# A three-layer CIN recommender on one core: layer 0 run three chunks further ahead of layer 1, its h in a ring of four, five of its chunks in the opening, TensorE's loop written out four times

## The reference

```
h = inputs                                   # [1024, 39, 16]
for i in 0, 1, 2:
    x = einsum('bhd,bmd->bhmd', h, inputs)   # outer product over fields
    x = einsum('bcd,oc->bod', x, W_i) + b_i  # 200 outputs
    x = relu(x)
    h, direct = x[:, :100], x[:, 100:]       # layer 2: direct = x
score = (sum over 16 of the directs, dense layers) @ fc_W + fc_b + biases
```

## Time and profile before

| what | us |
|---|---|
| median of three runs | 2750.92 |
| lowest, highest of them | 2747.41, 2753.69 |
| the profiled execution, its own time | 2752.34 |
| its span in the trace | 2750.5 |
| PE busy in that span | 2649.5 (96%) |
| granted TensorE clock, mean | 0.992 of full |

### The profile page before, as it was taken

The page is one execution under the profiler, slowest core; times in us unless marked ns, Lnnn a source line. Parts: engine busy times, 40 slices in busy tenths (PEclk is TensorE's granted clock), DMA queues, the critical chain, the costliest instruction groups (busy, mean ns, idle before and its releaser), DMA issues.

```text
span 2750.5 us, 66670 instructions
## 1 busy us (share of the span) xinstructions
PE 2649.5 (96%) x17928; PEld 2640.2 (96%) x17928; DVE 2285.0 (83%) x4584; ACT 1834.6 (67%) x4776; POOL 2249.6 (82%) x1912
## 2 busy tenths in 40 slices
PE   0699999999999999999999999999999999999999
PEld 0599999999999999999999999999999999999998
DVE  2788888888888888888888888888888888888884
ACT  0576776766767667676777767677677766766663
POOL 6788888888888888888888888888888888877763
PEclk9799999999999999999999999999999999999999
DMA  8844545445444454544545455454554545545441
GB/s 149 199 124 123 133 126 130 124 118 144 116 133 125 118 149 112 136 121 122 146 111 138 120 131 137 114 136 118 138 131 118 133 117 140 129 117 136 111 115 51
DMA packets 199914, 349.82 MB, mean 127 GB/s; under 512 B 66632, under 2 KB 118697, under 8 KB 199615
## 3 DMA queue, kind: packets, MB, share of 16 engines
q1 hardware_dynamic: 185782, 342.81, 45.6%
q0 software_dynamic: 10496, 2.88, 3.1%
q10 hardware_dynamic: 3464, 2.68, 0.3%
HBM read 344.29 MB, written 14.17 MB: 130 GB/s over the span
## 4 chain that ended last, share of the span: by engine, by line
PE 94%; POOL 2%; SPq 2%; DVE 1%; issue 1%; DMA 1%; ACT 0%; POOLq 0%; ACTq 0%; DVEq 0%
PE acc L642 61%; PE acc L643 28%; PE acc L667 2%; POOL raw L498 1%; PE hrep L678 1%; DVE W L1061 0%; SPq L319 0%; DMA odd<-lin 0%; PE acc L742 0%; PE acc L743 0%; PE acc L744 0%; SPq L309 0%; DMA raw<-table,idx 0%; PE hrep L764 0%; PE hrep L766 0%
## 5 line engine op out<-in xcount | busy, mean ns | idle before, releaser
L642 PE MATMUL acc<-W,xhi_d 128*128 128x400 f32 x5632 | 1732.4, 367 | 17.2 <-DVE xlo_d L1087 10.6
L643 PE MATMUL acc<-W,xlo_d 128*128 128x200 f32 x5632 | 1434.9, 255 | 0.0
L1087 DVE TENSOR_TENSOR xlo_d<-prod_d,xhi_d 128x512 fp32r<-128x512 f32 (+1 forms) x1536 | 983.9, 641 | 205.1 <-ACT xhi_d L819 147.2
L1079 DVE TENSOR_TENSOR prod_d<-hrep,xrep 128x512 f32<-128x512 f32 (+1 forms) x1536 | 1039.0, 677 | 105.8 <-issue 27.7
L548 POOL TENSOR_TENSOR xlo_p<-prod_p,xhi_p 128x512 fp32r<-128x512 f32 (+1 forms) x768 | 953.8, 1242 | 181.3 <-ACT xhi_p L813 135.6
L642 PEld LDWEIGHTS acc<-W,xhi_d 128*128 128x128 f32 x5632 | 1059.9, 188 | 20.1 <-DVE xlo_d L1087 12.9
L643 PEld LDWEIGHTS acc<-W,xlo_d 128*128 128x128 f32 x5632 | 1078.4, 191 | 0.0
L819 ACT ACTIVATE xhi_d<-prod_d 128x512 fp32r<-128x512 f32 (+1 forms) x1536 | 885.1, 577 | 222.6 <-PE acc L643 199.8
L642 PE MATMUL acc<-W,xhi_p 128*128 128x400 f32 x2944 | 917.2, 363 | 12.9 <-POOL xlo_p L548 12.9
L542 POOL TENSOR_TENSOR prod_p<-hrep_s,xrep 128x512 f32<-128x512 f32 x512 | 665.9, 1301 | 161.3 <-ACT hrep_s L856 108.5
L643 PE MATMUL acc<-W,xlo_p 128*128 128x200 f32 x2944 | 751.7, 255 | 0.0
(11 more groups left out here) (92 smaller groups left out, 927.1 us busy)
## 6 DMA issues: line engine op xcount, KB each, us to landing
xrep<-xs SPq DMA_DIRECT2D x384, 384.0 KB
l0x<-xs SPq DMA_DIRECT2D x378, 136.5 KB
xrep<-xs SPq DMA_DIRECT2D x384, 128.0 KB
xrep<-xs SPq DMA_DIRECT2D x128, 336.0 KB
xrep<-xs SPq DMA_DIRECT2D x128, 64.0 KB
l0x<-xs SPq DMA_DIRECT2D x378, 19.5 KB
lin<-w SPq DMA_DIRECT2D x8, 750.0 KB
raw<-table,idx POOLq DMA_INDIRECT x328
```

What stands on the lines that cost most here:

```text
L642: pe.matmul(bank[:, 0:2 * OUTS], hi, w, start=first, stop=last, skip_group_check=True)
L643: return pe.matmul(bank[:, 0:OUTS], lo, w[:, 0:OUTS], start=False, stop=last, skip_group_check=True)
L1079: nc.vector.tensor_tensor(to, h, xrep[:, (par + layer - 1) % 2, a:a + count, :], ALU.mult).then_inc(s_prod_d, 1)
L1087: op = nc.vector.tensor_tensor(xlo_d[:, slot, 0:split], bank[:, 0:split], xhi_d[:, slot, 0:split].bitcast(F32), ALU.subtract)
```

## The change

Layer 0 works on chunk i+4 in step i where it worked on chunk i+1. Its h goes to a ring of four SBUF slots, so a `take` waits for the transpose of three chunks earlier. PE's and ACT's loops have a body of four steps each (30 rounds), because the slot is a fixed address. The opening computes layer 0 of chunks 0 to 4, chunks 1 and 3 in the bank of layer 2; steps 124 to 127 have no layer 0. The odd buffer is one for both layers, so the load of layer 2's weights waits until layer 1's are split. ACT issues half of layer 2's DRAM rearrangement. In the opening SP loads layer 0's rows for chunks 2, 3 and 4 before layer 2's weights and those of chunk 5 behind them. Inputs of a tile are made ready one step earlier, with up to four gathers in a step instead of three. Six dimensions instead of four are scaled and turned first. The diff, cut to its core:

```diff
-EARLY = 4
+EARLY = 6
+LEAD = 3
+HRING = LEAD + 1
+OPENING = [(-4, 0), (-4, 1), (-3, 0), (-3, 1), (-2, 0), (-2, 1), (0, 2), (-1, 0), (-1, 1), (0, 3), (0, 0), (0, 1)]
+def chunk(layer, i):
+    return i + 1 + LEAD if layer == 0 else i + 1 - layer
-        hbuf = [sb("hbuf1", [P, P], F32), sb("hbuf2", [P, P], F32)]
+        hbuf = [sb("hbuf1", [P, HRING, P], F32), sb("hbuf2", [P, 1, P], F32)]
-        odd = [None, sb("odd1", [P, 3, OUTS], F32), sb("odd2", [P, 3, OUTS], F32)]
+        odd = [None] + 2 * [sb("odd", [P, 3, OUTS], F32)]
+        ROUNDS = (LAST - LEAD - 2) // HRING
+            if layer == 0 and isinstance(c, int) and c in (1, 3):
+                return acc[2]
...
             for e in (1, 2, 0, 3):
                 load_block(0, 0, e)
-            rows_of_weights(sp, 2, w2)
+            sp.wait_ge(s_prod_p, p_num(-3, 1) + 1)
+            load_layer0(2)
+            rows_of_weights(sp, 2, w2, (2, 3))
+            sp.wait_ge(s_prod_p, p_num(-2, 1) + 1)
+            load_layer0(3)
             sp.wait_ge(s_pt, 4)
-            sp.wait_ge(s_prod_p, p_num(0, 1) + 1)
-            load_layer0(2)
             for e in (1, 2, 0, 3):
                 sp.wait_ge(s_xblk[e], BLOCK_SEM[e])
                 load_block(1, 1, e)
+            sp.wait_ge(s_prod_p, p_num(-1, 1) + 1)
+            load_layer0(4)
+            sp.wait_ge(s_wlo, W_DONE[1])
             load_weights(sp, 2, w2)
+            sp.wait_ge(s_prod_p, p_num(0, 1) + 1)
+            load_layer0(5)
             sp.wait_ge(s_xt, 1)
             store_rows(0, EARLY, DIM - EARLY, s_xs)
...
-                    if j == 10:
+                    if j == 9:
                         store_inputs(k + 1)
-                    if j == 11:
                         store_dense_inputs(k + 1)
...
-            FREE_AT = 8
-            COUNTS = [2] * 5 + [3] * 9 + [2]
+            FREE_AT = 7
+            COUNTS = [1] + [2] * 6 + [3] * 6 + [4] * 2
...
             copy_idx(1, 1)
+            product(-4, 1, 0)
+            product(-4, 1, 1)
+            low(-4, 0)
+            low(-4, 1)
+            product(-3, 1, 0)
+            product(-3, 1, 1)
+            low(-3, 0)
+            low(-3, 1)
             pool.wait_ge(s_xin, 3)
-            gather(0)
+            for m in range(2):
+                gather(m)
+            product(-2, 1, 0)
+            product(-2, 1, 1)
+            low(-2, 0)
+            low(-2, 1)
+            for m in range(2, 4):
+                gather(m)
+            product(0, 0, 2)
             product(-1, 1, 0)
+            low(0, 2)
             product(-1, 1, 1)
             low(-1, 0)
             low(-1, 1)
+            product(0, 0, 3)
+            for m in range(4, 6):
+                gather(m)
             product(0, 0, 0)
+            low(0, 3)
             product(0, 0, 1)
             low(0, 0)
+            product(1, 1, 0)
             low(0, 1)
...
-            multiply(-1, "P", 0)
-            multiply(-1, "P", 1)
-            turn(0, 0, -1)
+            multiply(-4, "P", 0)
+            multiply(-4, "P", 1)
+            pe.wait_ge(s_l0c, 4)
+            multiply(-3, "P", 0)
+            multiply(-3, "P", 1)
+            turn(0, 0, 0, -1)
+            multiply(-2, "P", 0)
+            multiply(-2, "P", 1)
             multiply(0, "D", 0)
             multiply(0, "D", 1)
             multiply(0, "P", 2)
             multiply(0, "D", 2)
+            multiply(-1, "P", 0)
+            multiply(-1, "P", 1)
             multiply(0, "D", 3)
             multiply(0, "D", 4)
             multiply(0, "D", 5)
             multiply(0, "P", 3)
+            turn(0, 1, 1, 0)
+            multiply(0, "P", 0)
+            multiply(0, "P", 1)
-            with pe.Fori(2, LAST - 1) as i:
-                step(i)
+            with pe.Fori(0, ROUNDS) as k:
+                for j in range(HRING):
+                    step(k * HRING + (j + 2), (j + 2) % HRING)
...
             split_weights(0, 0)
-            high(-1, "P", 0)
-            high(-1, "P", 1)
-            high(0, "P", 0)
             split_weights(1, 0)
             split_weights(1, 1)
+            rows_of_weights(act, 2, w2, (0, 1))
+            split_weights(1, 2)
+            high(-4, "P", 0)
+            high(-4, "P", 1)
+            split_weights(1, 3)
+            split_weights(1, 4)
+            high(-3, "P", 0)
+            high(-3, "P", 1)
+            low_copy(0, 0, -4)
+            take(0, 0, 0)
             spread(0, 0, -1)
...
+            high(0, "P", 0)
             high(0, "P", 1)
+            low_copy(1, 0, 0)
             high(1, "P", 0)
             step(1, 1)
...
-            split_weights(1, [0, 1])
+            split_weights(1, [0])
             dve.wait_ge(s_fc, 32)
             evacuate(0, 0)
-            split_weights(1, [2])
+            split_weights(1, [1])
             product(0, 0, 0)
             product(0, 0, 1)
+            evacuate(0, 1)
+            split_weights(1, [2])
             product(0, 0, 2)
             low(0, 0)
-            split_weights(1, [3])
             product(0, 0, 3)
             low(0, 1)
-            split_weights(1, [4])
+            split_weights(1, [3])
             product(0, 0, 4)
             low(0, 2)
-            evacuate(0, 1)
+            evacuate(0, 2)
+            split_weights(1, [4])
             product(0, 0, 5)
```

More of the change, by code:

```diff
@@ L78, in present, with more @@
         return (0, 1, 2)
-    return tuple(n for n in range(3) if 0 <= i + 1 - n <= LAST)
+    return tuple(n for n in range(3) if 0 <= chunk(n, i) <= LAST)
+def more(i):
+    return not isinstance(i, int) or i < LAST
 def step_order(i):
@@ L86, in p_num @@
 def p_num(i, k):
-    if not isinstance(i, int):
-        return i * 6 + k
-    first = {-1: 0, 0: 2, CHUNKS - 1: 6 * (CHUNKS - 1) - 2, CHUNKS: 6 * CHUNKS - 6}
-    return first.get(i, 6 * i) + k
+    if isinstance(i, int) and i < 1:
+        return OPENING.index((i, k))
+    n, short = i * 6 + (k + 2 * LEAD), LAST - LEAD
+    if isinstance(i, int) and i >= short:
+        n -= 2 * (min(i, CHUNKS) - short) + (2 if i < CHUNKS else 2 + 2)
+    return n
 def d_num(i, d):
@@ L299, in pairs, with rows_of_weights @@
                 :, c * L0_SLOTS * L0_ROWS:(c + 1) * L0_SLOTS * L0_ROWS].rearrange("p (s r) -> p s r", r=L0_ROWS)
-        def rows_of_weights(engine, layer, src):
+        def rows_of_weights(engine, layer, src, quarters):
             used = H_QUARTER * FIELDS
             full = used // QUARTER
-            for q in range(4):
+            for q in quarters:
                 rows = lin[layer][used * q:used * (q + 1), :]
@@ L406, in step @@
             def step(i, buf):
-                if not isinstance(i, int) or i + 2 <= LAST:
+                if 0 in present(i) and 0 in present(i + 1):
                     sp.wait_ge(s_prod_p, p_num(i, 1) + 1)
                     waited()
-                    load_layer0(i + 2)
+                    load_layer0(chunk(0, i) + 1)
                 full = 2 in present(i)
@@ L591, in _ @@
             low(-1, 1)
+            product(0, 0, 3)
+            for m in range(4, 6):
+                gather(m)
             product(0, 0, 0)
+            low(0, 3)
             product(0, 0, 1)
             low(0, 0)
+            product(1, 1, 0)
             low(0, 1)
-            for m in range(1, 4):
-                gather(m)
-            product(0, 0, 2)
-            product(0, 0, 3)
-            low(0, 2)
-            for m in range(4, 7):
-                gather(m)
-            product(1, 1, 0)
-            low(0, 3)
-            for m in range(7, 9):
-                gather(m)
-            step(1, 1, 0, range(9, BEFORE))
+            step(1, 1, 0, range(6, BEFORE))
             with pool.Fori(0, TILES - 1) as k:
@@ L646, in multiply @@
                 layer, tiles = layer_of(kind, g), tiles_of(kind, g)
-                c = i + 1 - layer
+                c = chunk(layer, i)
                 if kind == "P":
@@ L655, in multiply @@
                 bank = bank_of(layer, c)
-                if first and bank is not acc[layer]:
+                if first and layer == 2 and bank is acc[0]:
                     pe.wait_ge(s_hbuf[0], CHUNKS)
+                elif first and layer == 2 and isinstance(c, int) and c == 0:
+                    pe.wait_ge(s_hbuf[0], 4)
+                elif first and layer == 0 and isinstance(c, int) and c < 5:
+                    if c >= 2:
+                        pe.wait_ge(s_hbuf[0], c - 1)
                 elif first and some(c):
@@ L671, in multiply, with turn @@
                 mm.then_inc(done, 1)
-            def turn(l, c, i):
+            def turn(l, c, slot, i):
                 pe.wait_ge(s_hbuf[l], c + 1)
@@ L689, in step @@
                     multiply(i, kind, g)
-                    if (kind, g) == ("D", 8) and layers == (1, 2):
+                    if (kind, g) == ("D", 8) and not more(i) and 1 in layers:
                         turn_last()
-                    if (kind, g) == ("P", 3) and 2 in layers and 0 in layers:
-                        turn(0, i + 1, i)
```

(22 more changed lines are left out.)

113 lines of the change are left out of this document (59 added, 54 removed).

## The result

The changed kernel takes **2790.44 us** (median of four runs, 2788.29 to 2793.04) beside 2750.24 for the kernel before on the same chip: ratio 1.0142, 95% interval 1.0130 to 1.0154, or 40 us slower. The profiled execution spans 2787.6 us against 2750.5, 37.1 more.

A forecast was written before the change was run, and what follows sets the result against it. TensorE, busy 96%, was taken as the bound, so only the ends could change: +9.7 opening, 0 steady, +1 tail, 0 loops, +10.7 us on the profiled 2752.3, or 2763; 2762 us on the median's scale, range 2744 to 2775.

The forecast's parts named there:

- Balance: Opening: D9 of step 1 ready at 144.3 us is break-even; each us later costs one, each earlier gives one.
- First high part: Opening, ACT: extra splits and DMA issues put its first high part near 74.3 us instead of 69.4.
- SP now waits for that last piece: Opening: SP's load of layer 2's weights waits for layer 1's last split, expected at 103 us.
- Load of layer 2: Opening, SP: issuing the thirteen DMAs of layer 2's weights takes 15 to 18.8 us, taken as 18.5.
- Chunk 5's rows: Opening: layer 0's rows for chunk 5, queued behind layer 2's weights, land at 127 us.
- P1 at 127 + 1.3 + 1.0 = 129.3 and step 1's P0 at 131.5: Opening, TensorE: after a stall from about 117 us it gets P1 at 129.3 and P0 at 131.5.
- POOL has ten gathers ... which leaves pauses; I take 154: Opening, step 1: POOL's pauses help DVE's splits; D9 ready between 152 and 158, taken as 154, +9.7 us.
- Four give 0.8 to 5.7 less the 1.4 of before ... I take +1: Tail: P5's low part behind POOL's product waiting for block 0, at four steps: -0.6 to +4.3 us, taken as +1.
- Loops 0: Written-out loops of TensorE and ACT: 0 to 60 us over 30 rounds, taken as 0.
- rival 3: TensorE's written-out loop waits 2.0 us at each of 30 returns, on top of the forecast: 2822 us; chance 0.11.
- Steady 0: Steady steps stay at 20.2 us: no change taken, 0 to 4 us if covers are thinner.
- 1 (the lead pays): Opening: D9 ready by 139 to 143 us, so the kernel is faster, typically 2743 to 2748 us; chance 0.24.

The follow-up runs named there:

- experiment 5: Changed kernel with TensorE's transpose of chunk 0 moved ahead of step 1 and ACT's take of chunk 4 right behind its low copy: 2780.90 us, ratio 1.0107 to the kernel before.
- experiment 7: Changed kernel with the edits of experiment 2, experiment 4, experiment 5 and experiment 6 together: 2755.16 us, ratio 1.0013 to the kernel before.
- experiment 1: Kernel before with only the loops of TensorE and ACT written out to four steps a round: 2755.78 us, ratio 1.0008 to the kernel before.
- experiment 2: Changed kernel; without layer 0 next, POOL makes P5's low part before P2's product, ACT makes P2's high part after D1: 2771.36 us, ratio 1.0065 to the kernel before.
- experiment 4: Changed kernel with SP loading chunk 5 of layer 0 ahead of its wait for layer 1's splits and layer 2's weights: 2776.93 us, ratio 1.0084 to the kernel before.
- experiment 6: Changed kernel with the five splits of layer 2's weights after D2 to D6 of step 1 instead of D4 to D8: 2782.91 us, ratio 1.0111 to the kernel before.
- experiment 11: Changed kernel with experiment 2, experiment 5 and experiment 6, and eight of layer 2's weight loads ahead of chunk 4's load: 2765.12 us, ratio 1.0047 to the kernel before.
- experiment 9: Changed kernel with chunk 5's load issued by ACT ahead of its spread of chunk 1, instead of by SP: 2785.18 us, ratio 1.0119 to the kernel before.
- experiment 12: As experiment 11, but with those eight loads between chunk 4's load and chunk 5's: 2758.34 us, ratio 1.0024 to the kernel before.
- experiment 10: Changed kernel with the edits of experiment 2, experiment 5, experiment 6 and experiment 9 together: 2756.70 us, ratio 1.0013 to the kernel before.

## Why the prediction was wrong

It gave 2762 us, 2744 to 2775; the result is 2790. The sign was right, and so were the two places of the loss: chunk 5 behind layer 2's weights, and P5's low part behind POOL's product in the tail. Against the sum of +10.7 us on the profiled execution, the opening cost 11.5 us more (21.2 instead of 9.7), the tail 17.8 more (18.8 instead of 1), the steady steps 2.8 less. Three steps failed: in the opening one wait was left out and 4 us of pauses were assumed; in the tail the price of one gap was taken for that of four.

- *Balance (right).* D9 of step 1 against 144.3 us: 165.4, so +21.1, as counted.
- *First high part (wrong, harmless).* Predicted 74.3, it was 70.13: ACT's DMA issues lay beside its own splits and cost it nothing. The first layer-0 matmul came at 72.14, not 76.
- *"SP now waits for that last piece" (wrong, partly offsetting).* The piece was done at 99.5, not 103, and SP did not wait for it: it was busy with chunk 4's issues until 101.41. *Load of layer 2.* 18.5 us predicted, 13.0 measured (101.5 to 114.5): the slow issue took 4.71 us, not 9.80. Why it was shorter wasn't tried. *Chunk 5's rows* at 123.6 instead of 127, P1 at 125.9 instead of 129.3. The new stall was foreseen, and is 10.4 us long. These 3.4 us in the forecast's favour hid part of the next error.
- *"P1 at 127 + 1.3 + 1.0 = 129.3 and step 1's P0 at 131.5" (**failed**).* P0 came 8.5 us behind P1, not 2.2. The step priced POOL's chain alone and left out that P0 of chunk 5 waits for the take of chunk 4, whose place in ACT's list the change had moved. It also let the splits wait for D0 and a free slot, where DVE in fact waited until 141.40 for the spread of h, behind P0. From P1 to the first split 18.1 us went by (125.86 to 143.97) instead of 8.3; less the 3.4 us above, the splits started at 144.0 instead of 137.6. Experiment 5, with the take and the transpose moved, gives what hung on this: 6.4 us of the opening.
- *"POOL has ten gathers ... which leaves pauses; I take 154" (**failed**).* 137.6 + 20.3 is 157.9; the 4 us taken off for pauses didn't exist. The splits and groups took 21.4 us, with 4.63 us again for the third split (152.56), as in the earlier trace rows; in experiment 7, where POOL ran a gather and no product or low part beside it, the third split took 1.82 (138.59). So 6.4 + 1.1 + 3.9 make the 11.4 us between 154 and 165.4.
- *Tail, "Four give 0.8 to 5.7 less the 1.4 of before ... I take +1" (**failed**, the largest error).* The place, the order of the lists and the number of steps were right. The price was 18.8 us. The bound multiplied the first gap by four. But the gaps were 1.87, 3.88, 3.77 and 2.61 us, 12.1 in all, and the clock fell behind the two long ones. That the first is short because it starts from full rings is the likeliest reading; it wasn't tried by itself. Also SP's block 0 stood behind blocks 1 and 2 for 4.2 us, and the earlier trace rows show it only from its issue on.
- *Loops 0 (right)*, by experiment 1 within 5 us: rival 3's 60 us is out, and no gap of TensorE stands anywhere between 200 and 2600 us, so at none of its returns. "ACT's return may cost it 2 us as well" came true: ACT idles 2.3 to 4.2 us at each of its returns, and its lead covers it. The Trainium skill (Runtime: NRT & Kernel Launch, section "Instruction fetch mechanics") lets a branch out of the fetched window wait for a fetch and gives TensorE room for 2048 instructions; the trace agrees for TensorE, with a body of some 1100. *Steady 0 (nearly right)*: -2.8 us, of which 2.0 are the one wait near 588 us that is gone; why it went wasn't tried.
- Of the rivals, 1 (the lead pays) was wrong even with the waits cured that experiments 2, 4, 5 and 6 found: experiment 7's opening is 7.5 us behind.

What stays open: whether any order would make the lead pay. A separate odd buffer alone wouldn't start the load sooner, since SP did not wait for the shared one; experiment 11 issued the bulk of it from 95.3 us, and chunk 4 came late. Starting it as early as before (90.5 us) wasn't tried. Nor were the earlier inputs, the fourth gather in a step and ACT's half of the rearrangement taken apart; what they cost or give lies in the 7.5 us that experiment 7's opening is behind.

## What to carry to other kernels

When a pipeline's depth changes, its last steps change shape too: walk through each list once for the steps in which a stage is missing, and ask of each wait who stands behind it. A stall that a trace shows once is no price for the same stall four times in a row: here the second and third were twice as long as the first, most likely because the buffers were no longer full. In the opening a longer lead moves small, urgent loads behind large ones in one queue, and none of the orders tried here gave both in time. And when the start of a piece of work is moved, ask again what runs beside it: the same split on DVE took 1.8 to 4.8 us.

## What was not expected of the hardware

- ACT's DMA issues overlap its own computing: four issues (65.64 to 68.6) ran while three splits (65.63 to 70.2) did, and the first high part lost nothing.

```profile
65.63 1.54 ACT L858 ACTIVATE W<-W 128x1600 fp32r<-128x1600 f32 x1 [17.25 <-DMA odd<-lin]
65.64 0.59 ACTq L330 DMA_DIRECT2D lin<-w  x1
...
70.13 1.03 ACT L867 ACTIVATE xhi_p<-prod_p 128x512 fp32r<-128x512 f32 x2
```

- A small load on another engine's queue still shares the way with a large one in flight: 8.7 us to use instead of 2.6 (experiments 9 and 4).
- Issues take longer behind a large one: three of 200 KB each took 10.35 us (experiment 11) and 6.78 us (experiment 12) behind one of 2.1 MB, and 2.62 us in the changed kernel, where 4.71 us had gone by on the issue between.
- Gaps can cost more than themselves: 8.1 us idle in 2640 to 2700 us, and 6 more at a granted clock of 0.50 behind two gaps of 3.8 and 3.9 us.
- DVE's split of 1.82 us, where it overlaps POOL's products and low parts, ends 1.7 us after POOL's low part, however long that takes: 4.63 and 3.80 us in the changed kernel, 4.75 in experiment 6, 4.04 in experiment 5, 3.96 and 2.38 in experiment 10.
- With four steps in its loop body ACT idles 2.3 to 4.2 us at each return. The profile names TensorE as the releaser in most rounds, POOL or nothing in others. But the gap comes in every round at the step with the return, and neither ACT with one step in the body (the kernel before) nor TensorE with four has such a gap. TensorE never waited for it. One return in the changed kernel:

```profile
329.39 0.52 ACT L867 ACTIVATE xhi_p<-prod_p 128x384 fp32r<-128x384 f32 x1 [2.93 <-issue]
```
